# A dilated depthwise convolution ahead of a spectral mixer: x blocks stationary and banded taps moving, with the image kept by eighths of the channels

## The reference

```python
# x: (64, 55, 55, 96) f32
k   = (raw_kernel * mask)        # 96 x 25 x 25; mask keeps every third row and column: 9 x 9 taps,
                                 # and not the one in the middle
lat = depthwise_conv(x, k, padding="SAME")       # one filter for each channel
x   = lat * x + bias + x

t = x as tokens                  # 64 items x 3025 tokens x 96
h = relu(bn1(ln(t) @ w1.T))      # 192 wide
X = fft(h over the tokens)       # then relu of a scaled real and imaginary part, inverse fft, real part
t = t + bn2(y @ w2.T)
t = t + ffn(ln(t))               # 96 -> 384 -> 96 in fp8 / f16 rounding
```

## Time and profile before

| | |
|---|---|
| median of 3 runs | 5371.43 us (5364.1 to 5374.72) |
| profiled execution, its own time | 5358.5 us |
| its span | 5356.7 us |
| TensorE busy | 4994.7 us (93%), 44874 instructions |
| VectorE busy | 4012.6 us (75%) |
| ScalarE busy | 3450.9 us (64%) |
| GpSimd busy | 2173.7 us (41%) |
| DMA | 898.68 MB, mean 168 GB/s |
| mean granted TensorE clock | 0.961 |

### The profile page before, as it was taken

One profiled execution on the slowest core, in us unless ns is written; L12 is line 12 of the kernel. 1 busy time (PEld: TensorE's weight loads), 2 busy tenths in 40 slices (PEclk: granted clock), 3 DMA queues, 4 the chain that ended last, 5 costly groups with the idle time before them and its releaser, 6 DMA issues.

```text
span 5356.7 us, 130067 instructions
## 1 busy us (share of the span) xinstructions
PE 4994.7 (93%) x44874; PEld 4550.5 (85%) x44874; DVE 4012.6 (75%) x11316; ACT 3450.9 (64%) x7242; POOL 2173.7 (41%) x2564
## 2 busy tenths in 40 slices
PE   8999999748999999999999999999999999999975
PEld 7999899727888888888888888888888888888863
DVE  4555566424788888888888888888888888888884
ACT  0000000016788888888888888888888888888852
POOL 0000000004455555555555555555555555555542
PEclk8999999858999999999999999999999999999985
DMA  7666666534666666666666666666666666666641
GB/s 240 184 183 184 181 177 182 151 81 128 172 174 177 177 179 168 176 171 174 174 179 180 168 175 172 174 175 174 182 169 174 172 174 177 175 178 170 164 113 33
DMA packets 730061, 898.68 MB, mean 168 GB/s; under 512 B 247825, under 2 KB 643914, under 8 KB 728202
## 3 DMA queue, kind: packets, MB, share of 16 engines
q1 hardware_dynamic: 658252, 801.02, 56.1%
q10 hardware_dynamic: 71174, 89.35, 5.4%
HBM read 505.60 MB, written 384.61 MB: 166 GB/s over the span
## 4 chain that ended last, share of the span: by engine, by line
PE 65%; DVE 7%; ACT 3%; issue 3%; DMA 1%; POOL 0%; DVEq 0%; POOLq 0%; SPq 0%
PE ps L983 11%; PE ps L1008 10%; PE ps L995 9%; PE ps L1024 6%; PE ps L1023 6%; PE ps L1035 5%; PE ps L1047 5%; PE ps L1073 4%; PE ps L1084 4%; PE ps L1060 3%; PE ps L1095 3%; ACT ps L753 1%; DVE gv L908 1%; ACT spec L748 1%; DVE mean L858 1%
## 5 line engine op out<-in xcount | busy, mean ns | idle before, releaser
L686 POOL TENSOR_SCALAR gv<-gv 96x400 f32<-96x400 f32 (+1 forms) x512 | 599.8, 1171 | 1741.3 <-DVE xn L923 1630.2
L709 POOL TENSOR_TENSOR tok<-tok,rstd 121x288 f32<-121x288 f32 (+1 forms) x512 | 350.5, 685 | 1259.2 <-DVEq L875 1259.2
L1008 PE MATMUL ps<-hid,fa 121*128 121x384 f32 (+1 forms) x2048 | 731.4, 439 | 71.8 <-DVE t L947 59.5
L983 PE MATMUL ps<-fb,acol 100*96 100x100 f32 x7936 | 773.8, 250 | 16.2 <-DVE spec L915 12.1
L800 ACT ACTIVATE y<-ps 128x1089 f16<-128x1089 f32 (+1 forms) x512 | 573.0, 1119 | 328.6 <-PE ps L1073 328.6
L983 PEld LDWEIGHTS ps<-fb,acol 100*96 100x96 f32 x7936 | 735.2, 164 | 28.2 <-issue 22.9
L286 DVE SCALAR_TENSOR_TENSOR xout<-cps,xin 114x351 f32<-114x351 f32 (+3 forms) x512 | 402.8, 787 | 435.1 <-PE cps L313 435.1
L995 PE MATMUL ps<-w1t,xnt 97*121 97x192 f32 x3200 | 703.1, 330 | 0.7 <-ACT xnt L791 0.7
L519 ACT ACT_TABLE_LOAD x1 | 1.3, 1283 | 1070.5 <-PEq L191 1070.5
L309 PE MATMUL cps<-xin,toep 114*114 114x117 f32 (+3 forms) x3072 | 613.9, 282 | 82.4 <-DMA xin<-in_x 68.9
L1023 PE MATMUL ps<-w2t,spec 97*100 97x96 f32 x3968 | 673.0, 251 | 4.1 <-ACT y L800 4.1
(11 more groups left out here) (103 smaller groups left out, 11599.7 us busy)
## 6 DMA issues: line engine op xcount, KB each, us to landing
a_d<-arow SPq DMA_DIRECT2D x448, 288.0 KB, 4.4
acol<-a_d SPq DMA_DIRECT2D x192, 600.0 KB
g_d<-mixed SPq DMA_DIRECT2D x256, 300.0 KB
tok<-x_d SPq DMA_DIRECT2D x64, 1134.4 KB
out<-o_sb SPq DMA_DIRECT2D x448, 136.1 KB
xin<-in_x SPq DMA_DIRECT2D x256, 211.5 KB, 5.6
grow<-g_d SPq DMA_DIRECT2D x128, 312.0 KB, 12.3
x_d<-xout ACTq DMA_DIRECT2D x144, 263.2 KB
```

The source lines that it names most:

```text
L686: nc.gpsimd.tensor_scalar(v, v, 0.0, None, ALU.max).then_inc(v_cut, 1)
L983: last = nc.tensor.matmul(COL[:, p, 0:Q], acol[:, p0 + p, hf * HH:(hf + 1) * HH], fb[:, p0 + p, :], start=True, stop=True)
L1008: nc.tensor.matmul(ps[0:M, ROW, 0:(s1 - s0) * H], fa[:, :], hid[part][:, 0:s1 - s0, :].rearrange("p j h -> p (j h)"), start=True, stop=Tru ...
```

## The change

The convolution's operands change places. The stationary operand is now a block of x: 114 pixels x 128 "items" (64 images x 2 halves of the rows). The moving operand is the banded taps. The result has the items on the partitions and pixels of a class along the free dimension, up to 18 x 19 of them.

- The work is cut into 8 eighths of 12 channels, and each into two passes (`t`): an even pass for the row classes 1 and 2 (the two halves of the partitions), an odd one for the row class 0, whose rows 0 to 9 and 10 to 18 stand in the two halves. A pass has 36 tiles (12 channels x 3 column classes) of three matmuls.
- x comes in twice: as `items`, the stationary blocks (SP's queue, a ring of 3 loads of 2 channels, each a DMA of 112 partitions and two of 1 partition), and as `images`, image rows for the gate (ACT's queue, 2 DMAs of 64 partitions a pass, straight into the buffer of the result, 4 passes deep).
- The taps of an eighth are loaded by SP's queue, two deep, instead of all at the start.
- VectorE gates in place; the bias moves to GpSimd (the last part of the last pass stays with VectorE), in parts of 5 or 6 rows.
- The stores are 2 DMAs of 64 partitions for each part, with runs of 55 x 12 numbers.
- `x1` in DRAM is kept as 8 channel eighths. The mixer therefore reads it in runs of 12 channels x tokens; `scale` reads the eighths and writes them as rows of 96 into a new pair of buffers `toks`; `residual` and `token_stats` read the eighths.

```diff
-CG = 3
-RING = 5
+E = 8
+EC = C // E
+CG = 2
+NG = EC // CG
+RING = 3
+ITEMS = 2 * B
+BLK = 3
+KINDS = ((0, 18, ((1, 0, 18), (0, 0, 10), (2, 8, 18))),
+         (HALO, 10, ((1, 4, 14), (0, 4, 10), (2, 8, 14))))
...
+        toep = [sb(f"toep{s}", [128, EC, TW]) for s in range(2)]
+        xin = [sb(f"xin{s}", [128, CG, DIL, BLK, ITEMS]) for s in range(RING)]
+        xo = [[sb(f"xo{k}{s}", [128, KINDS[k][1], R, EC]) for s in range(2)] for k in range(2)]
...
+            load_taps(0)
+            for t in range(PASSES):
+                e, k = t // 2, t % 2
                 for g in range(NG):
+                    n = t * NG + g
                     if n >= RING:
+                        sp.wait_ge(lat_done, STEP * (n - RING + 1))
+                    v = xin[n % RING][:, :, :, :, :].rearrange("p c x q i -> p (c x q i)")
+                    sp.dma_start(v[0:GK, :], xh[k, e * NG + g, 0:GK]).then_inc(x_in[n % RING], 16)
+                    for r in range(GK, GP):
+                        sp.dma_start(v[r:r + 1, :].rearrange("p (s n) -> p s n", s=16),
+                                     xh[k, e * NG + g, r:r + 1].rearrange("p (s n) -> p s n", s=16)).then_inc(x_in[n % RING], 16)
+                    if k == 0 and g == 3 and e + 1 < E:
+                        load_taps(e + 1)
...
+            def load_images(t):
+                e, k = t // 2, t % 2
+                if e >= 2:
+                    act.wait_ge(stored[k][e % 2], 32 * len(parts(k)) * (e // 2))
+                for n in range(2):
+                    nr, ys = image_rows(k, e, n, 0, KINDS[k][1])
+                    act.dma_start(xo[k][e % 2][n * B:(n + 1) * B, 0:nr, :, :].rearrange("p r x c -> p r (x c)"),
+                                  xi[e, :, ys].rearrange("b r x c -> b r (x c)")).then_inc(image_in[k][e % 2], 16)
...
+            for t in range(4):
+                load_images(t)
+            for t in range(PASSES):
+                for n in range(len(parts(t % 2))):
+                    store(t, n)
+                if t >= 1 and t + 3 < PASSES:
+                    load_images(t + 3)
...
+                for n in range(PER):
+                    m, xr = t * PER + n, n % DIL
+                    cols = len(range(xr, R, DIL))
+                    lat = ps[m % BANKS][:, 0:rows * GC].rearrange("p (r x) -> p r x", r=rows)[:, :, 0:cols]
+                    v = xo[k][e % 2][:, :, xr::DIL, n // DIL]
+                    dve.wait_ge(lat_done, m + 1)
+                    nc.vector.scalar_tensor_tensor(v, lat, 1.0, v, ALU.add, ALU.mult).then_inc(gated, 1)
...
+                    for i, (q, r0, r1) in enumerate(blocks):
+                        at = r0 - GR * q + GR
+                        last = nc.tensor.matmul(ps[m % BANKS][:, (r0 - o0) * GC:(r1 - o0) * GC],
+                                                xin[g % RING][0:GP, c % CG, xr, q, :],
+                                                toep[e % 2][0:GP, c, at * GC:(at + r1 - r0) * GC],
+                                                start=(i == 0), stop=(i == BLK - 1))
...
-        x1s = x1.rearrange("b y x c -> b (y x) c").rearrange("b (u s) c -> b u s c", u=U)
+        x1s = x1.rearrange("e b (u s) c -> b u e s c", u=U)
...
             def load_tokens(k):
                 if k >= 2:
-                    sp.wait_ge(turned, (k - 1) * NS)
-                sp.dma_start(tok[k % 2][:, :, 0:C], x1s[k]).then_inc(tok_in[k % 2], 16)
+                    sp.wait_ge(tok_scaled, (k - 1) * NS)
+                sp.dma_start(tok[k % 2][:, :, :, :].rearrange("p e s c -> p e (s c)"),
+                             x1s[k].rearrange("u e s c -> u e (s c)")).then_inc(tok_in[k % 2], 16)
...
             def scale(n):
                 k, (c0, c1) = n // NS, tokens(n)
                 pool.wait_ge(scale_ready, k + 1)
-                v = tok[k % 2][:, c0:c1, 0:C]
-                nc.gpsimd.tensor_tensor(v, v, rstd[k % 2][:, c0:c1].unsqueeze(2).broadcast_to([U, c1 - c0, C]),
+                if n >= 2:
+                    pool.wait_ge(turned, n - 1)
+                v = toks[n % 2][:, 0:c1 - c0, 0:C].rearrange("p j (e c) -> p j e c", e=E)
+                r = rstd[k % 2][:, c0:c1].unsqueeze(2).unsqueeze(3).broadcast_to([U, c1 - c0, E, EC])
+                nc.gpsimd.tensor_tensor(v, tok[k % 2][:, :, c0:c1, :].rearrange("p e j c -> p j e c"), r,
                                         ALU.mult).then_inc(tok_scaled, 1)
...
-                    last = nc.vector.bn_stats(bn[:, j, :], tok[k % 2][:, j, 0:C])
+                    last = nc.vector.bn_stats(bn[:, j, :], tok[k % 2][:, :, j, :])
...
-    x1 = nc.dram_tensor("x1_d", [B, R, R, C], F32).ap()
+    x1 = nc.dram_tensor("x1_d", [E, B, R * R, EC], F32).ap()
```

More of the change, by code:

```diff
@@ L31 @@
 HALO = KT // 2
-TROWS = GR + GR + HALO
+TROWS = 3 * GR
 TW = TROWS * GC
-CG = 3
-NG = C // CG
-RING = 5
-BANKS = 8
[L38 to L57, removed]
@@ new lines, with conv_items @@
+EC = C // E
+CG = 2
+NG = EC // CG
+RING = 3
+BANKS = 8
+ITEMS = 2 * B
+BLK = 3
+KINDS = ((0, 18, ((1, 0, 18), (0, 0, 10), (2, 8, 18))),
+         (HALO, 10, ((1, 4, 14), (0, 4, 10), (2, 8, 14))))
+def conv_items(x):
+    cols = [len(range(xr, R, DIL)) for xr in range(DIL)]
+    v = np.zeros((2, BLK * GR, GC, C, DIL, 2, B), np.float32)
+    for xr in range(DIL):
+        for n in range(2):
+            v[0, :, :cols[xr], :, xr, n] = x[:, n + 1::DIL, xr::DIL].transpose(1, 2, 3, 0)
+            rows = x[:, 0::DIL, xr::DIL].transpose(1, 2, 3, 0)
+            first = 10 * n - HALO
+            lo, hi = max(0, first), min(GC, first + BLK * GR)
+            v[1, lo - first:hi - first, :cols[xr], :, xr, n] = rows[lo:hi]
+    v = v.reshape(2, BLK, GR, GC, C // CG, CG, DIL, ITEMS)
+    return np.ascontiguousarray(v.transpose(0, 4, 2, 3, 5, 6, 1, 7)).reshape(2, C // CG, GP, CG * DIL * BLK * ITEMS)
@@ L211, in conv_stage @@
-        conv_done = sem("conv_done")
+        image_in = [[sem(f"image_in{k}{s}") for s in range(2)] for k in range(2)]
+        stored = [[sem(f"stored{k}{s}") for s in range(2)] for k in range(2)]
+        lat_done = sem("lat_done")
         gated = sem("gated")
[L214 to L222, removed]
@@ L224, in stored_before, with parts, on_dve, image_rows @@
-        def stored_before(u):
-            return sum(stores_of(UNITS[n]) for n in range(u % 2, u, 2))
+        biased = [sem("biased_pool"), sem("biased_dve")]
+        PASSES = 2 * E
+        PER = EC * DIL
+        STEP = CG * DIL
+        GK = GP // 16 * 16
+        LOADS = 16 * (1 + GP - GK)
+        def parts(k):
+            return [(n * 6, n * 6 + 6) for n in range(3)] if k == 0 else [(0, 5), (5, 10)]
+        def on_dve(t, n):
+            return t == PASSES - 1 and n == 1
+        def image_rows(k, e, n, r0, r1):
+            if k == 0:
+                y0, nr = DIL * r0 + n + 1, r1 - r0
+            else:
+                y0, nr = DIL * (10 * n + r0), min(r1, GC - 10 * n) - r0
+            return nr, slice(y0, y0 + DIL * (nr - 1) + 1, DIL)
@@ L228, in conv_stage, with biases_before @@
+        def biases_before(t, n):
+            return sum(len(parts(u % 2)) for u in range(t)) + n + 1
         block = ctx.enter_context(nc.Block())
@@ L245, in _ @@
[L245 to L260, removed]
@@ new lines, in store @@
+            def store(t, n):
+                e, k = t // 2, t % 2
+                r0, r1 = parts(k)[n]
+                if on_dve(t, n):
+                    act.wait_ge(biased[1], 1)
+                else:
+                    act.wait_ge(biased[0], biases_before(t, n))
+                for h in range(2):
+                    nr, ys = image_rows(k, e, h, r0, r1)
+                    act.dma_start(x1[e].rearrange("b (y x) c -> b y (x c)", y=R)[:, ys, :],
+                                  xo[k][e % 2][h * B:(h + 1) * B, r0:r0 + nr, :, :]
+                                  .rearrange("p r x c -> p r (x c)")).then_inc(stored[k][e % 2], 16)
@@ new lines, in _ @@
+            act.dma_start(cbias[:, :], cb.rearrange("(a c) -> a c", a=1).broadcast_to([128, C])).then_inc(cb_in, 16)
+            act.wait_ge(blank, 2)
+            for t in range(4):
[5 more added lines that the diff above has]
+                    load_images(t + 3)
+            for k in range(2):
+                for s in range(2):
+                    act.wait_ge(stored[k][s], 32 * len(parts(k)) * E // 2)
@@ new lines, in add_bias, with _ @@
+        def add_bias(engine, t, n):
+            e, k = t // 2, t % 2
+            r0, r1 = parts(k)[n]
+            v = xo[k][e % 2][:, r0:r1, :, :].rearrange("p r x c -> p (r x) c")
+            cbe = cbias[:, e * EC:(e + 1) * EC].unsqueeze(1).broadcast_to([128, (r1 - r0) * R, EC])
+            return engine.tensor_tensor(v, v, cbe, ALU.add)
+        @block.gpsimd
+        def _(pool):
+            for v in xo[1]:
+                nc.gpsimd.memset(v[B:2 * B, 9, :, :], 0.0).then_inc(blank, 1)
+            pool.wait_ge(cb_in, 16)
+            for t in range(PASSES):
+                pool.wait_ge(gated, PER * (t + 1))
```

(41 more changed lines are left out.)

48 lines of the change are left out of this document (22 added, 26 removed).

## The result

The changed kernel takes 5309.46 us (median of 4 runs, 5294.99 to 5312.82) against 5368.12 us: ratio 0.9886, interval 0.9867 to 0.9905. It is faster, by 1.1%; 5158 us was forecast, with 4965 to 5270 as the range, so the time lies 39 us above its upper end. The direction and the kind of limit were right, the size was not.

The account below looks back on a forecast made before the run. DMA was taken to bound the new convolution stage, ending at 861 us. Span 5356.7 - 209.5 (stage) - 4 (mixer) = 5143; with 1.8 and 12.9 for profiled time and median, 5158 us; range 4965 to 5270.

Parts of the forecast that it names:

- TensorE's work: Convolution: 2086 ns for an even and an odd tile together, x 288 = 601 us, against 1027 us today.
- the 15 ns on top of the columns: Convolution matmuls: a TensorE pass was taken to cost 15 ns plus 0.833 ns per moving column.
- So DMA is the bound, whatever else happens: Convolution: 266.3 MB, up from 197, would need 443 GB/s in TensorE's 601 us; the trace's most is 421.
- (114 and 128 partitions) at 421: Convolution: x items and taps, 117.6 MB, priced at 421 GB/s, 279 us.
- Half-wide transfers at 262: Convolution: new images and stores, 64 partitions each, 148.7 MB, priced at 262 GB/s, 568 us.
- 848 + 13: Convolution: 848 us of DMA (568 and 279) plus 13 us at the ends; stage ends at 861, 209.5 less.
- VectorE: Convolution gate: 755 and 487 ns, 358 us in all, hidden under TensorE's 601; effect 0.
- The mixer: Part behind the convolution: 4 us off for the first token load, the rest unchanged.
- the token load: Mixer's first load, in runs of 1200 B instead of 384: 8.5 us instead of 12.3, 4 taken off.
- The scale: Mixer, GpSimd: 24 rows of 12 instead of 3 of 96, at most +0.5 us a slot, hidden.
- slower than priced: Rival on convolution DMA, chance 0.24: everything at 288 GB/s, time 5235, or half-wide transfers at half of 421, time 5295.
- half-wide transfers at half of 421 without overlap: Convolution, a case of slower than priced: 706 + 279 us of DMA, stage 998, time 5295.

Follow-up runs that it names:

- The streams: A kernel without computation issuing the stage's transfers one kind after another: 128 partitions 384 to 401 GB/s, image halves 200, store halves 288, x items 232.

## Why the prediction was wrong

- **TensorE's work: right.** Loads of x follow each other freely at 7.31 us for six even tiles and 4.61 for six odd ones in the kernel after:

```profile
306.04 0.32 SPq L246 DMA_DIRECT2D xin<-in_items  x1
...
313.35 0.32 SPq L246 DMA_DIRECT2D xin<-in_items  x1
...
352.12 0.32 SPq L246 DMA_DIRECT2D xin<-in_items  x1
...
356.73 0.32 SPq L246 DMA_DIRECT2D xin<-in_items  x1
```

  That is (1.218 + 0.768) x 288 = 572 us for 601 forecast. Most of the difference is the 15 ns on top of the columns: the 288-column row gives 245 - 240 = 5, and with 5 the sum is 578.
- **"So DMA is the bound, whatever else happens": right.** Share 1.02, and every run that widened loads quickened the kernel. TensorE stood 246 us for VectorE behind the images, 31 us an eighth, as foreseen.
- **The step that failed: the x items "(114 and 128 partitions) at 421".** The 421 GB/s were measured on the old loads, which the host had padded to 128 partitions. The change drops the padding, and I carried the rate over to 112. The streams show 234: by that rate 100.8 MB cost 431 us instead of 239, +192 in the sum (an estimate, for x alone on the engines). Padding alone gave 107 us back (109 in the stage).
- **Half-wide transfers at 262: right in kind, somewhat high.** 200 for loads and 288 for stores: 372 + 258 = 630 us for 568, +62. Images full-width alone gave 112 us back (115 in the stage). The 262 came from one row, of stores that were narrow and had short runs as well, and it was used for loads and stores alike; that it lies between 200 and 288 is luck.
- **The sum** of the streams in line is then 848 + 192 + 62 = 1102; side by side (213 with images, 312 with stores) the same bytes make 133 / 0.213 + 133 / 0.312 = 1051; measured 1026.5 with both ends. With the right rates, adding one behind the other would have been 75 us too much and adding by pairs 25. In the forecast this hid a part of what the rates missed: the forecast's 848 + 13 ended 165 us too early, although the rates alone account for 254.
- **VectorE: right.** 777 and 504 ns for 755 and 487, although read and write are both strided; hidden. GpSimd's bias took 8562 ns for 3960 elements, 2.16 ns each, inside the bounds of 1.68 and 2.4.
- **The mixer: right, the figure in part by luck.** The part behind the stage is 4.1 us shorter for 4 forecast, but the token load gave only 2.0 of them (10.3 us where 8.5 was forecast). Over the six profiled executions with all loads, the changed kernel's and those of its wider versions, this part takes 4277 to 4284 us, so the rest is no more than their scatter. The scale takes 663 ns, 665 before, in spite of 24 short rows, the statistics 245 as before, and the stretch is unchanged.
- **Of the rivals** the second, "slower than priced", came nearest, in its case of half-wide transfers at half of 421 without overlap: stage 998 and 5295 us for 1026.5 and 5309. The images bear it out (200 GB/s). The stores, at 288, don't, and it too had x at 421: that it comes so near is luck.

## What to carry to other kernels

A rate belongs to the shape of the transfer it was measured on: when a change alters how many partitions a DMA spans, look for a row of that count, and take none from a neighbour. A load that is not 128 partitions wide ran, alone, at 188 to 267 GB/s here where 128 ran at 389. Padding 114 rows to 128 moved 12.4 MB more, some 32 us at 384 GB/s (an estimate), and still took 109 us off the stage. Two halves should be laid side by side by the host. Where the DMA share is 1, read GB/s beside it before calling the bandwidth used up.

## What was not expected of the hardware

Loads of 9216-byte rows: 120 partitions 211 GB/s, 104 partitions 188, both slower than 112 (267, and 236 in the streams) and 96 (246). Two half loads at once on two queues: 248 GB/s at 9216-byte rows, 332 at 2640. Stores from 64 partitions: 288 alone, and no cost that can be told beside wide loads (5004.91 against 5000.32 us). GpSimd's rows of 12 numbers cost no more than rows of 96 (663 and 665 ns for 288).
